# Conversion of the first feed-forward matrix in quarters, and other hand-over times for the start and the last two heads

## The chip, the cores and the metric

The kernel runs on one core of a Trainium2 chip. The metric is the device time of one execution in microseconds, the lower the better. The page and the trace are of one execution that the hardware profiler recorded. TensorE (PE) multiplies matrices, VectorE (DVE), ScalarE (ACT) and GpSimd (POOL) work on tiles in SBUF and PSUM, and SyncE (SP) issues the DMA transfers. PSUM has eight banks, and one matmul group fills one.

## What is computed

The input x is 16 sequences of 512 tokens with 256 features. A layer norm of x feeds an attention layer with 8 heads and a feed-forward net with three sign matrices, and both are added to x:

```python
def _L0_attn_ref(x, wq, wk, wv, wo):
    q, k, v = (einsum('bim,mhd->bhid', x, w) for w in (wq, wk, wv))
    q, k = rope(q), rope(k)
    s = einsum('bhid,bhjd->bhij', q, k) / 128
    s = s - 1e30 * (i < j)
    o = einsum('bhij,bhjd->bhid', softmax(s), v)
    return einsum('bhid,hdm->bim', o, wo)

def _L0_ffn_ref(x, k0, k1, k2, s0, s1, s2):      # k: booleans, True is 1 and False is -1
    h = concatenate([x, -x])                      # 256 -> 512 features
    h = relu(s0 * dense(k0, h)) * 2               # 512 -> 1024
    h = relu(s1 * dense(k1, h)) * 2               # 1024 -> 1024
    return s2 * dense(k2, h)                      # 1024 -> 256

xn = layernorm(x)
x = x + _L0_attn_ref(xn, ...) + _L0_ffn_ref(xn, ...)
```

## The kernel before

The kernel is one program of five instruction streams, written by Python code that runs once. Each stream is a `Queue` (L104), played in the order in which the code put things into it; an engine never takes a later instruction before an earlier one. Streams wait for each other by semaphores (`Queue.wait`).

**Units of work.** The batch entries b run from 0 to 15, and heads are counted through, g = 8 b + h, from 0 to 127. Every matmul group is a `Fill` (L467): it takes the PSUM bank that is planned to be free first, waits for the readers of what was in it, and issues its matmuls. For a head, `qk` (L585) makes q and k (two fills of 6 matmuls), `scores` (L636) the scores (three fills, 12 matmuls in all), `values` (L728) the product with v, called PV here (18 matmuls). Besides there are `v_proj`, `layer0`, `layer0_pair`, `layer1` (batch 0 only), the products of a Strassen scheme (`strassen`, L892) that take the place of layer 1 for the other batches, `layer2`, and the output projection (`proj`, `proj_last`). All numbers are kept as a high and a low f16 half, so most results are read twice: ACT makes the high half, DVE the low half by a subtraction.

**A head's chain behind its scores.** DVE adds the mask and takes the maxima (L659); ACT makes the bias (L667) and four exponentials, one for each 128 query rows (L673, tile p); DVE makes the inverse of the sums (L678, L680); POOL makes four high halves of the probabilities (L690, tile ph), DVE four low halves (L696, P_lo below); then SP issues two DMA transposes of ph into pt (`turned`, L699), and PV reads pt. For q and k, ACT swaps halves (L605, L606), DVE and POOL multiply by cos and sin, DVE adds (L618), ACT and DVE split (L624, L628).

**What sets the order.** PE's order is written by a loop over slots g (L1145): qk of head g + 2, then scores of head g + 1, then PV of head g - 1, with fillers between them. `PLACES` (L53) says for each filler its slot from the batch's first head and an order 0 to 5: 0 and 1 stand behind qk, 2 and 3 behind the scores, 4 and 5 behind PV. The order on the other engines follows from a clock that counts PE's work in units of a matmul of 512 columns: `at(delay, fn)` (L449) lets a step be written once the clock has moved by the delay. The delays are in `DELAY` (L96); the first three heads have their own in `EARLY` (L90), and steps that occur once at the start have absolute times in `SETUP` (L83). A step that someone needs earlier is pulled in front (`need`). `HELD` only guides the choice of banks.

**The start** (L1084). x of batch 0 is normalised on DVE, turned by PE into two banks (`first_T`, L548; eight matmuls of f32), and split by ACT and DVE into the tile xT. k0 arrives as bytes in the tile o. `subtract_k0` (L387, DVE) takes the difference of its halves for 512 of the 1024 columns into the fp8 tile w, and `sign_k0` (L394, ACT) multiplies by the sign of s0. `layer0(0, n)` (L763) multiplies the columns 128 n by xT; it waits for the half of w that it reads. `convert_k1` makes the 8 slices of the second matrix, five on POOL and three on ACT; `combine` (L419, POOL) and `block` (L411, ACT) make the seven fp8 operands WA of the Strassen scheme. `largest` and `powers` find powers of two by which the attention's weights are scaled, on DVE with two tiny matmuls each; `split_w` (ACT and DVE) then splits a part of a weight matrix. `last_load` (L258) is SP's wait for the differences of k0, since wo is loaded into the bytes' place.

## Time and profile before

| | us |
|---|---|
| median of 3 runs | 1779.78 |
| lowest and highest | 1779.66, 1780.92 |
| the profiled execution | 1781.45 |
| its span in the trace | 1779.6 |
| PE, DVE, ACT, POOL busy | 1723.5 (97%), 1535.5 (86%), 1269.1 (71%), 923.6 (52%) |
| chain that ended last: PE, DVE, DMA, ACT, POOL | 67%, 18%, 4%, 4%, 3% |

The profiled execution took 1.85 us more than its span, and it lies 1.67 us above the median. PE is busy nearly all the time, so the time is PE's work, at the clock it was granted, and the gaps in it. The timeline's rows give the start of a group of equal instructions, the time from its first start to its last end, and in brackets how long the engine had idled before and who ended that. Rows of a running group overlap by up to a tenth of a microsecond, since an engine takes the next instruction before the last has fully ended.

### The profile page before, as it was taken

To read this page: it belongs to the slowest core of one execution; us is meant where nothing else is said; L and a number is where in the kernel's file an instruction comes from. 1 tells how busy PE (TensorE), PEld (TensorE's weight loads), DVE (VectorE), ACT (ScalarE), POOL (GpSimd) and SP (SyncE) were. 2 spreads that over 40 slices of the span, in tenths; PEclk is the share of its full clock that TensorE was granted. 3 is DMA by queue.
4 is the path that set the end of the run, shared out by engine and by line. 5 is a ranking of instruction groups with operands and counts; after the bars stand their busy time and mean duration, and the time that the engine had idled before them with its cause. 6 is when DMAs were issued, how large, how long until landed. Compare 5 with 4: busy or idle time off the path is not lost.

```text
span 1779.6 us, 34027 instructions
## 1 busy us (share of the span) xinstructions
PE 1723.5 (97%) x12720; PEld 1196.4 (67%) x12720; DVE 1535.5 (86%) x3628; ACT 1269.1 (71%) x2715; POOL 923.6 (52%) x952
## 2 busy tenths in 40 slices
PE   6899989999999999999999999999999999999998
PEld 2456757767676676767767677676766767677667
DVE  8899888897988979898897988979889798888974
ACT  6777676777867678676776867778676776767773
POOL 6555544554545555455455545545455554555542
PEclk9999999999999999999999999999999999999999
DMA  5234543344343434334244433443533343343433
GB/s 171 48 55 72 94 68 78 66 82 80 55 96 63 80 66 72 78 66 96 56 87 73 66 78 66 84 78 55 96 66 78 66 72 82 63 95 59 80 65 66
DMA packets 454838, 134.08 MB, mean 75 GB/s; under 512 B 434704, under 2 KB 453648, under 8 KB 454672
## 3 DMA queue, kind: packets, MB, share of 16 engines
q1 hardware_dynamic: 454672, 131.90, 39.8%
q8 instruction: 100, 1.64, 0.4%
q14 instruction: 66, 0.54, 0.1%
HBM read 14.94 MB, written 8.39 MB: 13 GB/s over the span
## 4 chain that ended last, share of the span: by engine, by line
PE 67%; DVE 18%; DMA 4%; ACT 4%; POOL 3%; issue 3%; SPq 0%; DVEq 0%; POOLq 0%
PE bank L484 67%; DMA pt<-ph 3%; DVE ph L696 3%; DVE p L659 2%; DVE bank L618 2%; DVE bank L610 2%; DVE qk L628 2%; ACT p L673 2%; DVE rt L834 1%; DMA xT<-rt 1%; POOL tb L614 1%; POOL xT L316 1%; DVE v L538 1%; DVE hb L815 1%; DVE o L538 1%
## 5 line engine op out<-in xcount | busy, mean ns | idle before, releaser
L690 POOL TENSOR_SCALAR ph<-p,ri 128x384 f16<-128x384 f32 (+3 forms) x512 | 311.7, 609 | 453.5 <-DVE rk L680 416.2
L614 POOL TENSOR_TENSOR tb<-tb,sin 128x512 f32<-128x512 f32 x256 | 331.6, 1296 | 250.8 <-ACT tb L606 245.2
L484 PE MATMUL bank<-hb,wa 128*128 128x256 f16 x3360 | 379.7, 273 | 0.0
L484 PEld LDWEIGHTS bank<-hb,wa 128*128 128x128 fp8e5 x3360 | 328.0, 98 | 41.3
L673 ACT ACTIVATE p<-p,nm,sc 128x512 f32<-128x512 f32 (+3 forms) x512 | 328.6, 645 | 1.6
L696 DVE SCALAR_TENSOR_TENSOR ph<-p,rk,ph 128x512 f16<-128x512 f32 (+3 forms) x512 | 311.8, 616 | 0.0
L659 DVE CUSTOM_DVE_ANT_0 p<-bank,mask 128x512 f32<-128x512 f32 (+3 forms) x512 | 229.2, 485 | 51.1 <-PE bank L484 48.0
L484 PE MATMUL bank<-pt,v 128*128 128x256 f16 (+1 forms) x2304 | 234.0, 256 | 16.1 <-DMA pt<-ph 15.8
L484 PE MATMUL bank<-qk 128*128 128x512 f16 (+3 forms) x1536 | 231.4, 300 | 16.3 <-DVE qk L628 14.0
L484 PEld LDWEIGHTS bank<-pt,v 128*128 128x128 f16 x2304 | 203.3, 98 | 44.3 <-DMA pt<-ph 22.9
L484 PEld LDWEIGHTS bank<-qk 128*128 128x128 f16 x1536 | 133.3, 98 | 123.0 <-DVE qk L628 22.4
L624 ACT ACTIVATE qk<-bank 128x512 f16<-128x512 f32 x256 | 151.1, 591 | 78.2 <-DVE bank L618 77.8
L628 DVE TENSOR_TENSOR qk<-bank,qk 128x512 f16<-128x512 f32 x256 | 175.1, 684 | 29.5 <-ACT qk L624 28.2
L618 DVE TENSOR_TENSOR bank<-bank,tb 128x512 f32<-128x512 f32 x256 | 177.9, 695 | 17.3 <-POOL tb L614 12.4
L484 PE MATMUL bank<-wv,xT 128*128 128x512 f16 x768 | 183.7, 379 | 3.9 <-DMA xT<-rt 3.8
L605 ACT ACTIVATE tb<-bank 64x512 f32<-64x512 f32 x256 | 152.2, 594 | 49.3 <-PE bank L484 42.0
L484 PE MATMUL bank<-xT,wk 128*128 128x512 f16 x768 | 186.7, 379 | 0.3 <-DVE v L538 0.3
L484 PE MATMUL bank<-xT,wq 128*128 128x512 f16 x768 | 186.7, 379 | 0.0
L610 DVE TENSOR_TENSOR bank<-bank,cos 128x512 f32<-128x512 f32 x256 | 177.2, 692 | 5.0 <-ACT tb L606 4.9
L484 PE MATMUL bank<-wo,o 128*128 128x256 f16 x1536 | 173.1, 273 | 0.0
L844 POOL TENSOR_TENSOR hb<-rt,hb 128x1024 f16<-128x1024 f32 x60 | 132.3, 2205 | 61.7 <-ACT hb L840 60.5
L484 PEld LDWEIGHTS bank<-wo,o 128*128 128x128 f16 x1536 | 150.4, 98 | 20.6
(107 smaller groups left out, 2265.5 us busy)
## 6 DMA issues: line engine op xcount, KB each, us to landing
out<-xnat SPq DMA_DIRECT2D x32, 256.0 KB, 2.3
xnat<-in_x SPq DMA_DIRECT2D x15, 512.0 KB, 3.9
pt<-ph SPq DMA_TRANSPOSE x256, 4.3
o<-in_k SPq DMA_DIRECT2D x1, 1024.0 KB, 7.8
v<-in_wq SPq DMA_DIRECT2D x1, 1024.0 KB, 9.8
v<-in_wk SPq DMA_DIRECT2D x1, 1024.0 KB, 11.6
ph<-in_wv SPq DMA_DIRECT2D x1, 1024.0 KB, 14.0
o<-in_wo SPq DMA_DIRECT2D x1, 1024.0 KB, 10.8
```

Of the source, the lines that this page charges most:

```text
L484: self.todo.append(lambda e, stop=False: e.matmul(self.ps[:, cols[0]:cols[1]], lhsT, rhs, start=first, stop=stop, skip_group_check=skip))
L605: act.put(lambda e: e.activation(TB[0:64, r, :], f.ps[64:128, :], ACT.Copy))
L610: done["straight", n] = dve.put(lambda e: e.tensor_tensor(f.ps[:, :], f.ps[:, :], COS[:], ALU.mult))
L614: done["crossed", n] = pool.put(lambda e: e.tensor_tensor(tb, tb, SIN[:], ALU.mult))
L618: done["rot", n] = dve.put(lambda e: e.tensor_tensor(f.ps[:, :], f.ps[:, :], tb, ALU.add))
L624: done["qk_hi", n] = act.put(lambda e: e.activation(hi, f.ps[:, :], ACT.Copy))
L628: done["qk_lo", n] = dve.put(lambda e: e.tensor_tensor(lo, f.ps[:, :], hi, ALU.subtract))
L659: done["max", g, i] = dve.put(lambda e, i=i, a=a, w=w: e.tensor_tensor_reduce(out=P[:, r, S_OFF[i]:S_OFF[i] + w], in0=f.ps[:, a:a + w], in ...
L673: done["exp", g, i] = act.put(lambda e: e.activation(v, v, ACT.Exp, bias=NM[:, g % 4, i:i + 1], scale=SC[:, 0:1], accum_out=SM[:, g % 4, i ...
L690: done["P_hi", g, i] = pool.put(lambda e: e.tensor_scalar(part(r, i, HI), v, RI[:, g % 4, i:i + 1], 4096.0, ALU.mult, ALU.mult))
L696: done["P_lo", g, i] = dve.put(lambda e: e.scalar_tensor_tensor(part(r, i, LO), v, RK[:, g % 4, i:i + 1], part(r, i, HI), ALU.mult, ALU.su ...
L844: done["h0t", b, i] = pool.put(lambda e: e.tensor_tensor(HB[:, 3:7, LO, i, :], RT[:, 4:8], HB[:, 3:7, HI, i, :], ALU.subtract))
```

## The change

The edits are these.

1. k0 is converted in four quarters of 256 columns, each with its own event, in place of two halves. The signs of the three scales are made before the normalised x is written. The first quarter is subtracted right after that, and its sign is put on ACT between the first and the second high half of xT; the three others follow both halves of xT on DVE and on ACT. `layer0(0, n)` waits for quarter n // 2. SP's load of wo waits for all four differences.
2. `SETUP`, `EARLY` and the places of the fillers of batch 0, of a pair of layer 0 and two Strassen parts of batch 1, and of two fillers of the last batch have other numbers.
3. A table `LATE` gives the last two heads, 126 and 127, delays of their own for nine steps.

```diff
 PLACES = {
-    "l0_1": ((2, 2), (3, 0), (4, 4), (5, 2)),
+    "l0_1": ((2, 2), (3, 0), (3, 5), (5, 2)),
...
-    "seg_15": ((2, 0), (3, 4), (4, 1), (4, 2), (5, 2), (5, 2), (5, 5), (6, 5)),
+    "seg_15": ((2, 0), (3, 4), (4, 1), (4, 2), (5, 2), (5, 4), (5, 5), (6, 5)),
...
+LATE = dict(rotated=14.1, qhi=19.3, qlo=22.0, bias=4.9, exp=11.3, inv=19.6, high=36.1, low=33.0, turned=46.4)
...
-            sp.wait(done["k0_diff", 0], done["k0_diff", 1])
+            sp.wait(*[done["k0_diff", n] for n in range(4)])
...
+        def quarter(v, n):
+            return v.rearrange("p (c n) -> p c n", c=2)[:, :, n * 256:n * 256 + 256]
+
+        def subtract_k0(n):
 
             dve.wait(done["k_in", 0])
-            done["k0_diff", half] = dve.put(lambda e: e.tensor_tensor(
-                W0[:, :, half * 512:half * 512 + 512], halves(K0S[:, 0:2048], half), halves(K0S[:, 2048:4096], half),
+            done["k0_diff", n] = dve.put(lambda e: e.tensor_tensor(
+                W0[:, :, n * 256:n * 256 + 256], quarter(K0S[:, 0:2048], n), quarter(K0S[:, 2048:4096], n),
                 ALU.subtract, saturate=False))
 
+        def sign_k0(n):
+
+            act.wait(done["k0_diff", n], done["signs"])
+            w0 = W0[:, :, n * 256:n * 256 + 256]
+            done["W0", n] = act.put(lambda e: e.activation(w0, w0, ACT.Copy, scale=SG[:, 0:1], saturate=False))
...
-            return EARLY[name][g] if g < 3 and name in EARLY else DELAY[name]
+            if g < 3 and name in EARLY:
+                return EARLY[name][g]
+            return LATE[name] if g >= G - 2 and name in LATE else DELAY[name]
...
                 split(f, XT[:, 0, HI, :, c, :], XT[:, 0, LO, :, c, :], ("xT_hi", c), ("xT", 0, c))
+                if c == 0:
+                    at(DELAY["hi"], lambda: sign_k0(0))
...
-            pe.wait(done["W0", n // 4])
+            pe.wait(done["W0", n // 2])
...
         norm(0)
+        signs()
         norm_apply(0)
-        signs()
         subtract_k0(0)
-        sign_k0(0)
         ffn_scales()
-        subtract_k0(1)
-        last_load()
         first_T()
         while later:
             later.pop(0)[1]()
-        sign_k0(1)
+        for n in range(1, 4):
+            subtract_k0(n)
+            sign_k0(n)
+        last_load()
```

What the tables do to the order is seen on three engines.

The first place is ACT at the start, from the first conversion of k0 (w<-w,sg) to the first products of layer 1 (h<-bank). wa are the Strassen operands, wq and wk the first split parts of the weights. Before:

```order
L398 ACTIVATE w<-w,sg 128x2x512
L530 ACTIVATE xT<-bank 128x4x128 x2
L398 ACTIVATE w<-w,sg 128x2x512
L408 ACTIVATE hb<-o,sg 128x1024
L408 ACTIVATE rt<-o,sg 128x1024 x2
L530 ACTIVATE hb<-bank 128x512 x8
L416 ACTIVATE wa<-hb 128x1024
L416 ACTIVATE wa<-rt 128x1024
L530 ACTIVATE h<-bank 128x512
L360 ACTIVATE wq<-v,kn 128x2x256
L360 ACTIVATE wk<-v,kn 128x2x256
L416 ACTIVATE wa<-hb 128x1024 x2
```

and now:

```order
L535 ACTIVATE xT<-bank 128x4x128
L401 ACTIVATE w<-w,sg 128x2x256
L535 ACTIVATE xT<-bank 128x4x128
L401 ACTIVATE w<-w,sg 128x2x256 x3
L411 ACTIVATE hb<-o,sg 128x1024
L411 ACTIVATE rt<-o,sg 128x1024 x2
L535 ACTIVATE hb<-bank 128x512 x8
L419 ACTIVATE wa<-hb 128x1024
L419 ACTIVATE wa<-rt 128x1024
L419 ACTIVATE wa<-hb 128x1024 x2
L535 ACTIVATE h<-bank 128x512
L363 ACTIVATE wq<-v,kn 128x2x256
```

The first high half of xT stands ahead of any conversion, and three quarters stand ahead of the conversion of k1 (hb<-o,sg and rt<-o,sg) where one half stood. Two of the operands wa have moved ahead of h, wq and wk.

The second place is PE behind the PV of head 2 (bank<-pt,v; the last of its four rows is shown). xT,w is a pair of layer 0 of batch 1, w,h is layer 2 of batch 0, and xT,wq and xT,wk are q and k of head 6. Before:

```order
L484 MATMUL bank<-pt,v 128x128 x3
L484 MATMUL bank<-xT,wq 128x512 x6
L484 MATMUL bank<-xT,wk 128x512 x6
L484 MATMUL bank<-wv,xT 128x512 x6
...
L484 MATMUL bank<-w,h 128x256 x32
L484 MATMUL bank<-xT,w 128x512 x8
L484 MATMUL bank<-wv,xT 128x512 x6
```

and now:

```order
L489 MATMUL bank<-pt,v 128x128 x3
L489 MATMUL bank<-xT,w 128x512 x8
L489 MATMUL bank<-xT,wq 128x512 x6
L489 MATMUL bank<-xT,wk 128x512 x6
L489 MATMUL bank<-wv,xT 128x512 x6
...
L489 MATMUL bank<-w,h 128x256 x32
L489 MATMUL bank<-wv,xT 128x512 x6
```

The third pair of layer 0 has moved ahead of head 6's q and k. The rows left out end with the PV of head 3 in both.

The third place is DVE at the end, between the last inverse but one (head 126; ri and rk) and the maxima of head 127 (ISA p,mx). The ph rows are the P_lo, the two first here of head 125 and the four next of head 126; bank<-bank,rt and h<-bank,h belong to the Strassen scheme of batch 15, o<-bank,o to the PV of head 124. Before:

```order
L696 SCALAR_TENSOR_TENSOR ph<-p,rk,ph 128x256
L696 SCALAR_TENSOR_TENSOR ph<-p,rk,ph 128x128
L535 SCALAR_TENSOR_TENSOR h<-bank,h 128x2x256
L696 SCALAR_TENSOR_TENSOR ph<-p,rk,ph 128x512
L538 SCALAR_TENSOR_TENSOR o<-bank,o 128x512
L696 SCALAR_TENSOR_TENSOR ph<-p,rk,ph 128x384
L889 TENSOR_TENSOR bank<-bank,rt 128x512
L659 ISA p,mx<-bank,mask 128x512
...
L659 ISA p,mx<-bank,mask 128x256
L659 ISA mx 128x1
L535 SCALAR_TENSOR_TENSOR h<-bank,h 128x2x256
L696 SCALAR_TENSOR_TENSOR ph<-p,rk,ph 128x128
```

and now:

```order
L703 SCALAR_TENSOR_TENSOR ph<-p,rk,ph 128x256
L703 SCALAR_TENSOR_TENSOR ph<-p,rk,ph 128x128
L543 SCALAR_TENSOR_TENSOR o<-bank,o 128x512
L703 SCALAR_TENSOR_TENSOR ph<-p,rk,ph 128x512
L703 SCALAR_TENSOR_TENSOR ph<-p,rk,ph 128x384
L703 SCALAR_TENSOR_TENSOR ph<-p,rk,ph 128x256
L540 SCALAR_TENSOR_TENSOR h<-bank,h 128x2x256
L896 TENSOR_TENSOR bank<-bank,rt 128x512
L703 SCALAR_TENSOR_TENSOR ph<-p,rk,ph 128x128
L666 ISA p,mx<-bank,mask 128x512
```

The last P_lo of head 126, on which its DMA transposes wait, stood behind all four maxima of head 127 and two rows more, and stands ahead of the first of them now. On PE the PV of head 124 moves ahead of 32 matmuls of the Strassen scheme, and on ACT a copy of that scheme (bank<-bank, L875) moves from ahead of head 126's bias to between the high halves of q and the first exponential. Between the two ends, from head 9 to head 123, the rows of all five engines are the same in both kernels but for the numbers of the banks.

## Rows read from the trace of the kernel before

**Rows 1.** Three stretches: length, busy us per engine (count), granted clock, DMA share, GB/s.
```profile
0.00:170.00 170.00, 145.08 (x839) 80.67 (x840) 150.91 (x326) 122.74 (x240) 96.02 (x102) 0.97 0.38 87
170.00:1740.00 1570.00, 1544.67 (x11586) 1087.01 (x11585) 1367.16 (x3264) 1136.81 (x2454) 822.02 (x842) 1.00 0.41 74
1758.00:1760.00 2.00, 2.00 (x13) 1.51 (x12) 0.00 (x0) 0.00 (x0) 0.00 (x0) 0.50 0.00 0
```

**Rows 2.** Timeline of PE, last heads: start us, duration us, instructions, idle before them.
```profile
1747.56 1.82 PE L484 MATMUL bank<-pt,v 128*128 128x256 f16 x18
...
1750.96 3.66 PE L484 MATMUL bank<-w,h 128*128 128x256 fp8e5 x32
...
1757.15 3.32 PE L484 MATMUL bank<-pt,v 128*128 128x256 f16 x18 [2.53 <-DMA pt<-ph]
...
1760.26 6.92 PE L484 MATMUL bank<-wo,o 128*128 128x256 f16 x60
```

**Rows 3.** Timeline, the issue of the last three pairs of DMA transposes by SyncE.
```profile
1742.00 3.72 SPq L707 DMA_TRANSPOSE pt<-ph  x2
...
1750.24 3.74 SPq L707 DMA_TRANSPOSE pt<-ph  x2
...
1763.04 3.70 SPq L707 DMA_TRANSPOSE pt<-ph  x2
```

**Rows 4.** Timeline of ScalarE, VectorE and GpSimd between 1735 and 1750 us.
```profile
1735.60 0.58 ACT L875 ACTIVATE bank<-bank 128x512 f32<-128x512 f32 x1
...
1740.94 0.17 DVE L678 RECIPROCAL ri<-sm 128x4 f32<-128x4 f32 x1
...
1741.41 3.05 POOL L690 TENSOR_SCALAR ph<-p,ri 128x512 f16<-128x512 f32 x4 [1.28 <-DVE rk L680]
...
1742.82 0.83 DVE L696 SCALAR_TENSOR_TENSOR ph<-p,rk,ph 128x512 f16<-128x512 f32 x1
...
1749.87 0.34 DVE L696 SCALAR_TENSOR_TENSOR ph<-p,rk,ph 128x128 f16<-128x128 f32 x1
```

**Rows 5.** Timeline of the start: x transposed, k0's signs, the first matmuls, GpSimd's combinations.
```profile
7.45 1.94 PE L489 MATMUL bank<-ident,rt 128*128 128x128 f32 x8 [7.45 <-DVE rt L316]
...
9.72 1.15 ACT L398 ACTIVATE w<-w,sg 128x1024 fp8e5<-128x1024 fp8e5 x1 [7.50 <-DVE w L390]
...
10.77 1.06 ACT L530 ACTIVATE xT<-bank 128x512 f16<-128x512 f32 x2
...
12.25 9.13 PE L484 MATMUL bank<-xT,w 128*128 128x512 f16 x32 [2.86 <-DVE xT L538]
...
17.68 4.20 POOL L428 TENSOR_TENSOR wa<-hb 128x1024 fp8e5<-128x1024 f16 x2 [0.41 <-POOL hb L405]
```

**Rows 6.** Timeline, from the first powers of two to the maxima of wo and wv.
```profile
24.00 1.95 DVE L342 TENSOR_SCALAR dg<-ident,ar 128x2 f32<-128x2 f32 x1
...
28.09 2.35 POOL L428 TENSOR_TENSOR wa<-wa,hb 128x1024 fp8e5<-128x1024 fp8e5 x1
...
28.48 2.50 DVE L362 SCALAR_TENSOR_TENSOR wk<-v,kn,wk 128x512 f16<-128x512 f32 x1
...
35.20 2.28 DVE L322 TENSOR_REDUCE p<-ph 128x1 f32<-128x2048 f32 x1
...
37.53 0.80 PE L484 MATMUL bank<-ident,p 128*128 128x128 f32 x2 [3.72 <-DVE p L322]
...
38.12 5.33 PE L484 MATMUL bank<-hb 128*128 128x512 f16 x12
```

**Rows 7.** Timeline, heads 2 to 7, where a pair of layer 0 moves.
```profile
115.71 0.18 DVE L678 RECIPROCAL ri<-sm 128x4 f32<-128x4 f32 x1 [0.96 <-ACT p L673]
...
116.66 1.81 PE L484 MATMUL bank<-pt,v 128*128 128x256 f16 x18
...
132.15 1.82 PE L484 MATMUL bank<-pt,v 128*128 128x256 f16 x18 [0.78 <-DMA pt<-ph]
...
139.40 1.79 PE L484 MATMUL bank<-qk 128*128 128x512 f16 x12 [1.54 <-DVE ri L678]
```

19 lines of the change are left out of this document (6 added, 13 removed), and 28 rows, old and new, of the table PLACES.

## Prediction

> **What bounds the kernel now.** I read first the table of stretches [rows 1]. From 170 to 1740 us PE is busy for 1544.67 of 1570 us at a clock of 1.00, and there the change moves nothing: only PE's work could make that part shorter. In the first 170 us PE is idle for 170 - 145.08 = 24.9 us, while DVE is busy for 150.91. So the start is set by DVE, ACT and POOL as much as by PE, and a gap that is closed there can come back at the next one. The end is the other place. The timeline of PE's last heads [rows 2] shows one wait that nothing makes good later: PV of head 126 stands for 2.53 us until its DMA transposes have landed, starts at 1757.15 us, and PE works without a gap from there to its last matmul. After the wait PE runs at a granted clock of 0.50 [rows 1], its lower level of 1.2 GHz: the 18 matmuls of this PV take 3.32 us where those of head 125 took 1.82 [rows 2].
>
> **The end, part by part.** The transposes of head 126 are issued from 1750.24 us [rows 3], directly behind P_lo of its last tile, which starts on DVE at 1749.87 [rows 4]. All its high halves were ready by 1741.41 + 3.05 = 1744.46 [rows 4]. So some 5 us of DVE's order, not its inputs, lie between. In the new order that P_lo stands ahead of head 127's maxima.
>
> When it runs now: a copy of the Strassen scheme, 0.58 us at 1735.60 on ACT [rows 4], ran where ACT had nothing else to do. It now stands between the first high half and the exponentials of head 126, so these end 0.5 us later, the inverse moves from 1740.94 to 1741.4, and POOL's four high halves end at 1744.9. On DVE there follow the last two P_lo of head 125, the low half of o, three P_lo of head 126 (the first was 0.83 us), a low half of h1, and an addition that waits for ACT's third copy. I add these to 1741.4 and come to about 1746.0 us for the last P_lo, 3.9 us earlier. From the issue to the PV that waited, head 125 took 1747.56 - 1742.00 = 5.6 us and head 126 6.9 us [rows 2, 3]. The transposes then land at 1751.9 to 1753.3.
>
> When PE comes: layer 2 starts at 1750.96 and takes 3.66 us [rows 2], so PE was ready for this PV at 1754.6. The late exponentials cost something here. The two late P_lo of head 125 move its transposes by 0.45 us, and since its PV followed them directly, PE comes 0.45 us later to all that follows; the copy that opens the next Strassen part costs about the same 0.5 us at the same place, and the two waits overlap. So PE comes at 1755.05, with 1.7 us in hand at worst. The wait of 2.53 us goes.
>
> With it goes the slow clock: 3.32 - 1.82 = 1.50 us on this PV, and, until the clock is back, an estimated 0.17 us on the first of the 60 matmuls behind it (6.92 us) [rows 2]. Sum: -2.53 - 1.50 - 0.17 + 0.45 = -3.75 us. What is late next is PV of head 127. Its transposes were issued at 1763.04 in a kernel that was 2.1 us behind, and only its last P_lo waits now for the low half of o of head 126, which follows PV by 2.4 us. That gives an issue near 1758.3 and a landing at 1763.9 to 1765.2, for a PV that PE reaches at about 1766.5 behind its projection and layer 2. The cover is 1.3 us at worst. Bounds of this part: 0 if the hand-over fails, -4.2 if the 0.45 us is not paid.
>
> **k0 in quarters.** The turned x leaves PE at 7.45 + 1.94 = 9.39 us, but ACT took a half of w (1.15 us) first and began on xT at 10.77; the first matmul waited for xT's low half until 12.25 [rows 5]. Now ACT begins near 9.5. A high half is 1.06 / 2 = 0.53 us; a quarter of w I take as half of 1.15, 0.6 us, with 1.15 as its upper bound if all of it were fixed cost. DVE's low half of about 0.6 us then ends near 10.8, and PE starts at 10.9: 1.35 us earlier. Behind that the lead shrinks. ACT now has three quarters in front of k1's conversion where it had one half, so its part of k1 ends near 17.6 us and not 16.3, and the high halves of the first layer start there. The seventh fill of layer 0 reuses the bank of the first and waits for that. PE ends layer 0 some 0.8 us earlier, not 1.35. POOL's combinations need all eight slices of k1, and began at 17.68 [rows 5], so they stay where they are or move by 0.1.
>
> And POOL pins what follows. A scaling of two columns on DVE (dg, L342) took 1.95 us, and the low half of the first part of wk 2.50 us [rows 6], while a POOL combination ran from 28.09 for 2.35 us; neither ended before POOL's instruction did. These two stand in the chain to the largest value of wv, which DVE finds at 35.20 to 37.48, and for which PE waits 3.72 us [rows 6]. If DVE reaches dg or wk 0.5 us earlier, it waits 0.5 us longer for the same POOL instruction. I take 0 for the whole lead at 37.5 us, between +0.3 (POOL moves) and -2.1, one POOL instruction less in the chain.
>
> The Trainium skill states this as a rule, in "SBUF — State Buffer", in its section "SBUF: two separate sides": DVE and GpSimd share one pair of ports as an exclusive lock, held for the whole instruction, and the loser fully blocks. By it the lead of 1.35 us is worth nothing as long as POOL's row of combinations stands still, and the trace agrees (2.50 us for wk). If the two shared bandwidth instead, the sum at 37.5 us would be about -0.8.
>
> **The other numbers at the start.** Two of ACT's fp8 operands move into a gap of ACT; q's part 2 and 3 of wq, the third low half of qk, wo's low halves and the low half of h1 change places on DVE. DVE is busy from 48.9 to 74 us but for its waits on POOL and ACT, and the same instructions stand in front of every wait of PE but the next two; I take 0, between +0.5 and -0.7, one low half (about 0.7 us) earlier in front of the scores of head 1.
>
> **The pair of layer 0** comes earlier on PE by the scores of head 5, PV of head 3 and layer 2. DVE's 0.96 us of idleness at 115.71 [rows 7] stays, since it waits there for ACT. The pair's two banks are freed only by DVE's last low half of it. With ACT's two rows and DVE's four differences and two low halves behind the inverse of 115.71 that is at 119.9 us. PV of head 3 takes one of these banks. It ran at 116.66 [rows 7] and, behind the pair's 8 matmuls (12 of the scores took 1.79 us), would now come at 118.4, so it gets a wait of 1.5 us that is not there today. P_lo of head 4 come 1.2 us later, so PV of head 4, at 132.15 after 0.78 us of waiting, waits until 133.4. But the scores at 139.40, which waited 1.54 us [rows 7], do so for DVE: in front of them stands the same work but one P_lo of 128 columns (0.34 us for such a one in [rows 4]), so they come at 139.0. PE's delay is absorbed there. I take -0.45 for the start as a whole, between +2 and -3.
>
> **The sum.** The profiled execution took 1781.45 us. It becomes 1781.45 - 3.75 - 0.45 = 1777.25. The median of the runs is 1.67 us lower, so the forecast is 1775.6 us, 0.24% less. A measurement of this kernel tells apart about 0.2%, 3.56 us.
>
> **Rivals.**
> *The start takes part of it back.* The new wait of PV 3 and the longer one of PV 4 are not absorbed, because ACT, too, is fuller behind the pair. 1.5 + 1.2 us of waits less the 0.45 above give +1 to +2 there, and 1777.5 us (1776.3 to 1778.8). For it: DVE is the fuller engine in this stretch, and nothing in the row at 139.40 shows how ACT stands. Against: the same work stands in front of 139.40.
> *A new wait at the end.* The hand-over is moved, and the 18 matmuls wait for another thing: the transposes of head 127, whose cover is only 1.3 us, or a larger loss at head 125. With the slow clock once more that gives back 2 to 3 us: 1778.3 us.
> *More than forecast.* DVE's dg slips in front of a POOL instruction, the maximum of wv comes up to 2 us earlier, and PE's wait of 3.72 us shrinks so far that the clock stays up behind it. Then the 12 matmuls at 38.12, which took 5.33 us behind the wait [rows 6], take about half of that. I take 2.5 us off in all: 1773.1 us.
> *Slower than before.* PV 3's wait is longer than I think, 4 us or more, because the pair's last low half is queued behind the maxima of head 5; PE falls to 1.2 GHz behind it as at 1757, and the chains of heads 5 and 6 start later by as much. It decides from a loss of 3.75 us at the start: 4 us of wait and 1.5 us of slow clock leave +1.75, 1781.5 us.
>
> The Trainium skill, "TensorE: Matmul & The Clock Gate", section "HAM oscillation — how this bites in real kernels", describes a kernel in which each wait for a DMA sends the matmuls behind it to half clock. Here the waits of 3.72 and 2.53 us agree with it, and that of 1.54 us does not show it. [...]
>
> **How the numbers follow.** Forecast 0.42, with its own range 1774.3 to 1777.0; start takes part back 0.28; new wait at the end 0.12; more than forecast 0.13; slower 0.05. Faster by over 3.56 us, below 1776.2: most of the first (0.39), all of the fourth (0.13), a little of the second (0.03), 0.55. Slower by over 3.56 us: 0.03. Within: 0.42. The range runs from 1772.8 to 1778.7: it leaves out the slower case, half of the new wait, and the lower part of the fourth, 0.17 together.
>
> **What would show it.** Right: no idle time before the PV of head 126, its 18 matmuls in 1.8 us, the issue of its transposes near 1746 us on today's scale; the first matmul of layer 0 at 10.9 us, the wait for the maximum of wv ending at 37.5 +- 0.3 us; a wait of some 1.5 us before PV 3. The prediction is wrong if PE waits at head 125 or 127 for over 1 us, if the maximum of wv comes before 36.5, or if the scores of head 7 start after 140 us.

## The result, and the profile after

The changed kernel takes 1774.49 us (median of 7 runs, 1773.84 to 1776.89), the kernel before 1779.78 us (7 runs, 1777.15 to 1780.92). The ratio is 0.9973, with a 95% interval of 0.9962 to 0.9985: 5.3 us less, where 4.2 were forecast. The profiled execution took 1775.91 us and has a span of 1774.1 us.

The stretches of [rows 1] in the kernel after (the third is now the one in which the PV of head 126 runs):

```profile
0.00:170.00 170.00, 142.64 (x842) 79.72 (x843) 149.72 (x329) 122.73 (x243) 98.09 (x102) 0.99 0.39 88
170.00:1740.00 1570.00, 1545.06 (x11599) 1088.13 (x11598) 1368.40 (x3265) 1136.41 (x2456) 821.83 (x842) 1.00 0.41 74
1753.00:1755.00 2.00, 2.00 (x24) 1.83 (x22) 1.49 (x3) 0.00 (x0) 1.24 (x3) 1.00 0.00 0
```

PE is idle for 170 - 142.64 = 27.4 us of the first 170 (24.9 before) and yet has got further by then, since less of its work fell into stretches at 1.2 GHz. The end, on PE, as in [rows 2]:

```profile
1746.41 1.81 PE L489 MATMUL bank<-pt,v 128*128 128x256 f16 x18
...
1753.31 1.81 PE L489 MATMUL bank<-pt,v 128*128 128x256 f16 x18
1754.95 6.71 PE L489 MATMUL bank<-wo,o 128*128 128x256 f16 x60
...
1764.99 1.81 PE L489 MATMUL bank<-pt,v 128*128 128x256 f16 x18
```

The wait before the PV of head 126 is gone, and its 18 matmuls take 1.81 us. The chain ahead of it, as in [rows 3, 4] (GpSimd's high halves, DVE's last low half P_lo, and SyncE's transposes of heads 126 and 127):

```profile
1740.29 3.85 POOL L697 TENSOR_SCALAR ph<-p,ri 128x512 f16<-128x512 f32 x4 [1.59 <-DVE rk L687]
...
1745.10 0.34 DVE L703 SCALAR_TENSOR_TENSOR ph<-p,rk,ph 128x128 f16<-128x128 f32 x1
...
1745.47 3.70 SPq L714 DMA_TRANSPOSE pt<-ph  x2
...
1756.77 3.72 SPq L714 DMA_TRANSPOSE pt<-ph  x2
```

The start, as in [rows 5, 6]. ScalarE's signs of the quarters, DVE's subtractions, GpSimd's five slices of k1 and its row of combinations, and the chain to the maximum of wv:

```profile
10.64 7.37 PE L489 MATMUL bank<-xT,w 128*128 128x512 f16 x24 [1.29 <-DVE xT L543]
...
11.50 2.76 DVE L393 TENSOR_TENSOR w<-o 128x512 fp8e5<-128x512 uint8 x3
...
13.09 1.95 ACT L401 ACTIVATE w<-w,sg 128x512 fp8e5<-128x512 fp8e5 x3 [2.23 <-DVE w L393]
...
10.16 7.36 POOL L408 TENSOR_SCALAR hb<-o,sg 128x1024 f16<-128x1024 uint8 x5 [3.35 <-DMA o<-in_k]
18.61 4.21 POOL L431 TENSOR_TENSOR wa<-hb 128x1024 fp8e5<-128x1024 f16 x2 [1.09 <-ACT rt L411]
...
26.83 2.12 POOL L431 TENSOR_TENSOR wa<-hb,rt 128x1024 fp8e5<-128x1024 f16 x1
29.03 2.35 POOL L431 TENSOR_TENSOR wa<-wa,hb 128x1024 fp8e5<-128x1024 fp8e5 x1
...
24.31 0.51 DVE L345 TENSOR_SCALAR dg<-ident,ar 128x2 f32<-128x2 f32 x1
...
27.22 2.29 DVE L365 SCALAR_TENSOR_TENSOR wq<-v,kn,wq 128x512 f16<-128x512 f32 x1 [0.79 <-ACT wq L363]
29.43 2.50 DVE L365 SCALAR_TENSOR_TENSOR wk<-v,kn,wk 128x512 f16<-128x512 f32 x1
...
38.48 0.80 PE L489 MATMUL bank<-ident,p 128*128 128x128 f32 x2 [3.72 <-DVE p L325]
39.06 4.16 PE L489 MATMUL bank<-hb 128*128 128x512 f16 x12
```

And PE at heads 3, 4 and 7, as in [rows 7]:

```profile
120.43 1.80 PE L489 MATMUL bank<-pt,v 128*128 128x256 f16 x18 [1.40 <-DVE hb L822]
...
133.87 1.82 PE L489 MATMUL bank<-pt,v 128*128 128x256 f16 x18 [0.89 <-DMA pt<-ph]
...
139.41 1.79 PE L489 MATMUL bank<-qk 128*128 128x512 f16 x12
```

**Where the time went.** The start of each head's PV in PE's timeline serves as a time mark along the kernel. The table gives it for one profiled execution of each kernel, in us against the kernel before (minus is earlier), with the duration of the PV of head 126 in brackets where it was slow. The experiments below stand in the same table. Medians and ratios are against runs of the kernel before on the same chip: its medians there were 1780.05 us (end_only, start_only, plo_back, k1_first), 1780.46 us (quarters_only, pair_back, warm, fetch) and 1779.90 us (the last four rows).

| kernel | head 0 | 7 | 12 | 17 | 123 | 125 | 126 | 127 | median us | ratio, interval |
|---|---|---|---|---|---|---|---|---|---|---|
| before, absolute | 83.37 | 164.35 | 229.53 | 302.49 | 1727.79 | 1747.56 | 1757.15 (3.32) | 1770.51 | 1779.78 | |
| after | +0.42 | -0.60 | -0.57 | -0.87 | -1.43 | -1.15 | -3.84 | -5.52 | 1774.49 | 0.9973, 0.9962 to 0.9985 |
| end_only | -0.07 | -0.08 | +0.03 | -0.09 | -0.75 | -0.46 | -3.16 | -4.83 | 1776.97 | 0.9988, 0.9979 to 0.9997 |
| start_only | +0.15 | -0.85 | -0.74 | -0.81 | -1.11 | -1.14 | -1.14 (2.91) | -1.15 | 1778.50 | 0.9996, 0.9988 to 1.0005 |
| plo_back | -1.35 | -2.37 | -2.25 | -2.52 | -3.61 | -3.33 | -3.44 (3.38) | -3.44 | 1777.81 | 0.9991, 0.9982 to 1.0000 |
| quarters_only | -0.90 | -0.88 | -0.77 | -0.82 | -1.10 | -1.13 | -1.13 (3.31) | -1.29 | 1780.03 | 0.9998, 0.9988 to 1.0007 |
| pair_back | -0.05 | -0.05 | -0.03 | -0.33 | -1.18 | -0.90 | -3.60 | -5.27 | 1776.30 | 0.9978, 0.9969 to 0.9987 |
| k1_first | -1.71 | -2.73 | -2.66 | -2.86 | -2.38 | -2.08 | -4.77 | -6.44 | 1774.72 | 0.9973, 0.9964 to 0.9982 |
| warm | -1.17 | -2.23 | -2.19 | -5.15 | -4.03 | -3.74 | -6.44 | -8.11 | 1772.68 | 0.9961, 0.9948 to 0.9973 |
| fetch | +0.14 | +0.14 | +0.16 | -3.16 | -5.59 | -5.62 | -6.93 | -8.59 | 1772.71 | 0.9957, 0.9944 to 0.9971 |
| whole_block | -0.44 | -0.40 | -0.30 | -0.17 | -0.16 | -0.19 | -0.16 (3.19) | -0.45 | 1780.63 | 1.0007, 0.9998 to 1.0016 |
| after_44 | -1.44 | -2.44 | -2.41 | -4.00 | -5.68 | -5.39 | -8.08 | -9.75 | 1770.92 | 0.9950, 0.9934 to 0.9965 |
| k1_44 | +0.48 | -0.56 | -0.55 | -3.66 | -6.15 | -5.86 | -8.55 | -10.23 | 1769.65 | 0.9946, 0.9934 to 0.9959 |
| k1_88 | -0.17 | -0.13 | -0.03 | -1.62 | -2.00 | -0.83 | -3.53 | -5.20 | 1775.76 | 0.9973, 0.9963 to 0.9982 |

Of the 5.52 us that the kernel after is ahead at head 127, 0.60 were gained by head 7, 0.83 between heads 7 and 123, where the rows are the same from head 9 on, and 4.09 behind head 123.

### The profile page after: what moved, and what is told of

Same layout as the page of the kernel before. It is cut to its first block, busy times and chain, and to the rows that moved or that the text cites. A ratio compares the mean times of both kernels' runs of the same rounds, so it can differ in the third digit from the quotient of the medians.

```text
span 1774.1 us, 34030 instructions
## 1 busy us (share of the span) xinstructions
PE 1718.2 (97%) x12720; PEld 1194.3 (67%) x12720; DVE 1534.4 (86%) x3630; ACT 1267.5 (71%) x2717; POOL 925.6 (52%) x952
## 3 DMA queue, kind: packets, MB, share of 16 engines
q8 instruction: 100, 1.64, 0.4%
## 4 chain that ended last, share of the span: by engine, by line
PE 67%; DVE 19%; ACT 5%; DMA 3%; POOL 3%; issue 2%; SPq 0%; DVEq 0%; POOLq 0%; ACTq 0%
PE bank L489 67%; DVE ph L703 3%; DVE p L666 3%; DVE bank L625 3%; DVE bank L617 2%; DVE qk L635 2%; DMA pt<-ph 2%; ACT p L680 2%; DVE rt L841 1%; POOL xT L319 1%; DVE v L543 1%; DMA xT<-rt 1%; POOL tb L621 1%; DVE hb L822 1%; DVE o L543 1%
## 6 DMA issues: line engine op xcount, KB each, us to landing
v<-in_wk SPq DMA_DIRECT2D x1, 1024.0 KB, 10.9
o<-in_wo SPq DMA_DIRECT2D x1, 1024.0 KB, 10.2
```

## The experiments

**Two halves of the change.** end_only is the kernel before with the table LATE (its line of numbers is left out of the cut) and these places; start_only is the kernel after without all of them:

```diff
-    "seg_15": (..., (5, 2), (5, 2), (5, 5), (6, 5)),
+    "seg_15": (..., (5, 2), (5, 4), (5, 5), (6, 5)),
-    "l2_15": ((8, 0), (7, 0)),
+    "l2_15": ((8, 2), (7, 0)),
-            return EARLY[name][g] if g < 3 and name in EARLY else DELAY[name]
+            if g < 3 and name in EARLY:
+                return EARLY[name][g]
+            return LATE[name] if g >= G - 2 and name in LATE else DELAY[name]
```

> The kernel before with only the change at the end: the table of distances for the last two heads, and the new places of the second Strassen scheme and of layer 2 in the last batch. The start is that of the kernel before. Theory: the end is worth the same without the new start, since nothing ties the two: no wait before the PV of head 126, its 18 matmuls in 1.8 us and not 3.3, and PE's end 4.1 us earlier counted from the PV of head 123 (2.69 of wait, 1.68 of slow clock, less 0.28 that the exponentials cost). In time 3.8 to 4.2 us less than the kernel before, ratio 0.9977. Rival: part of it comes from the start, in that the heads arrive at the end in another rhythm; then the wait stays over 0.5 us and the ratio is above 0.9985.

Measured: from head 123 to 127 PE gains 4.08 us, as in the kernel after (4.09). The wait is gone, so the rival falls. The median is 3.1 us lower, but the interval of the ratio (0.9979 to 0.9997, or 0.5 to 3.7 us) reaches neither the 4.1 us of the profile nor the ratio of 0.9977 that was forecast. The kernel before spreads from 1776.8 to 1781.8 us here. It may be that its faster executions lose less at the end than the profiled ones do; none of those was profiled, so this is not shown.

> The changed kernel without the end: last two heads, Strassen scheme and layer 2 of the last batch as in the kernel before. Theory: only the start's share remains, 0.6 to 0.9 us by the PV of head 17 (PE at 301.6), and a ratio of 0.9995 (0.9990 to 1.0). The wait of 2.5 us and the 3.3 us of the 18 matmuls at head 126 are back. Between the PVs of heads 17 and 121 the rows are the same in every kernel, so what these 1399 us differ by is scatter of single executions. Rival: the 0.76 us that the changed kernel gained there comes from its start (another phase of the transfers against the engines); then this kernel shows 1398.6 to 1398.7 there once more and the kernel with the new end alone 1399.4.

Measured: 0.85 us by head 7 and 0.81 by head 17, median 1.6 us lower, and the wait of head 126 and its slow matmuls are back. The middle, from head 17 to 121, took 1399.42 us before, 1398.66 after, 1398.77 in end_only, 1398.87 here, 1398.50 in plo_back and 1399.61 in k1_first. That follows neither the start nor the end, so the 0.8 us that the kernel after gained there is scatter of single executions. The two halves add up within such scatter: 3.1 + 1.6 us against 5.3 us.

**One instruction.** plo_back is the kernel after with the last P_lo of head 126 back behind the maxima of head 127:

```diff
-                at(delay("low", g) + n * DELAY["low_i"], lambda i=i: low(i))
-            at(delay("turned", g), turned)
+                at(delay("low", g) + n * DELAY["low_i"] + (10 if g == G - 2 and i == 0 else 0), lambda i=i: low(i))
+            at(delay("turned", g) + (10 if g == G - 2 else 0), turned)
```

> The changed kernel with one DVE instruction moved back: the last low half of P of head 126 stands behind the maxima of head 127 and one low half of h1 again, 0.34 us of work. Theory: this one instruction carries the gain at the end. It starts near 1748.6 us instead of 1745.1, its transposes are issued at 1748.9 and land 5.5 us later at the earliest, so the PV that PE reaches at 1753.3 waits for at least 1.1 us; with the slower landings that the kernel before shows (5.1 and 6.0 us per transpose) for 2.7 us and at 1.2 GHz, 4.1 us in all. Rival: the wait at head 126 came from the whole row of DVE or from ACT's copy ahead of the exponentials; then this kernel is within 0.5 us of the changed one.

The timeline of DVE, SyncE and PE, and then, from the view of tile pt, the landings of these two transposes (least, median and most us from issue):

```profile
1746.34 0.34 DVE L703 SCALAR_TENSOR_TENSOR ph<-p,rk,ph 128x128 f16<-128x128 f32 x1
...
1746.71 3.77 SPq L714 DMA_TRANSPOSE pt<-ph  x2
...
1753.71 3.38 PE L489 MATMUL bank<-pt,v 128*128 128x256 f16 x18 [2.42 <-DMA pt<-ph]
```

```profile
DMA to landing us min/median/max: 5.2/5.7/6.1
```

The wait is 2.42 us and the PV slow; from head 123 to 127 nothing is gained. In this order of the instructions the place of one instruction of 0.34 us, with the transposes that must follow it, decides on the whole gain at the end. It also left a question: the two transposes landed 6.1 and 5.2 us from issue, and those of the kernel after 4.3 and 3.8.

**Why they land late.** The DMA engines in 40 slices of 0.2 us, before (1750 to 1758 us), with the queues in the half microsecond from 1754.0:

```profile
DMA  0000000799999999999999990000006990000000
GB/s 0 0 0 0 0 0 0 151 223 215 209 209 212 220 220 216 212 193 192 205 220 291 129 29 0 0 5 9 9 9 146 289 200 0 0 0 0 0 0 0
...
q8 instruction: 1, 0.02, 11.7%
```

At slice 21, counted from 0, one packet of 16 KB with instructions passes (q8, with its MB and its share). The transposes had moved some 210 GB/s; from slice 23 on they move 0 to 29 for seven slices, 1.4 us. The kernel fetch has 44 more matmuls on PE while it waits for x; whole_block has 128:

```diff
             fs = [Fill(("T", c)) for c in range(2)]
+            for _ in range(44):
+                pe.put(lambda e: e.matmul(fs[0].ps[:, 0:2], ID[:].bitcast(F16)[:, 0:128],
+                                          ID[:, 0:2].bitcast(F16)[:, 0:2], start=True, stop=True), signal=False)
```

> The kernel before with 44 matmuls of 2 columns more on PE, in the 7.4 us in which it waits for x; they are not read. They move nothing but PE's place in its own instruction stream, by 88 instructions. Theory: the transposes of head 126 landed late (5.1 and 6.0 us from issue, where others need 3.6 to 4.3), because a block of PE's instructions was loaded at 1754.4 us over the same DMA engines: from 1754.5 to 1756 they moved 4 to 37 GB/s and not 204. Here that block is loaded about 5 us earlier, between the transposes of heads 125 and 126. Then they land 3.6 to 4.3 us from issue, and the wait before the PV of head 126 is 1.0 to 1.3 us and not 2.53. Rival: the late landing comes from the place, for instance from what else runs there; then the landings stay at 5.1 and 6.0 us and the wait at 2.5.

The same views of fetch, 7 us earlier in the execution (1743 to 1751 us), and its PV of head 126:

```profile
DMA  0020000000000069999999999999999981000000
GB/s 0 0 82 0 0 0 0 0 0 0 0 0 0 0 146 223 211 211 210 223 210 220 223 212 188 200 200 229 210 207 223 201 168 18 0 0 0 0 0 0
```

```profile
DMA to landing us min/median/max: 3.8/4.1/4.3
```

```profile
1750.22 1.82 PE L484 MATMUL bank<-pt,v 128*128 128x256 f16 x18 [1.22 <-DMA pt<-ph]
```

and the PV of head 13, before and in fetch:

```profile
244.29 2.59 PE L484 MATMUL bank<-pt,v 128*128 128x256 f16 x18 [3.50 <-DMA pt<-ph]
```

```profile
243.16 1.82 PE L484 MATMUL bank<-pt,v 128*128 128x256 f16 x18 [2.21 <-DMA pt<-ph]
```

The packet passes ahead of the transposes of head 126 (slice 2). These run through and land 3.8 and 4.3 us from issue, PE waits 1.22 us, and the clock stays up. The kernel before has become 7.7 us faster, by instructions that compute nothing. In the profile 3.0 us of this lie at the end (head 123 to 127). Another 3.3 us lie between heads 12 and 17, where the wait for the transposes of head 13 fell from 3.50 to 2.21 us and 1.7 us of slow clock behind it went. These two transposes landed 5.5 and 6.0 us from issue before, with a packet of instructions at 241.5 to 242 us and 1 GB/s in the half microsecond behind it, and 4.2 and 4.3 us from issue here. The last 2.4 us lie in the middle, and no run takes them apart. The next packet now meets the transposes of head 127, which land 5.0 and 6.2 us from issue; PE comes to them late enough and does not wait.

> The kernel before with 128 matmuls of 2 columns more on PE at the start, where 44 gave 7 us. Theory: the loads of PE's instructions come in equal blocks: 100 of them with 1.64 MB for PE's some 25,500 instructions in the kernel before, so one per about 256. 128 matmuls with their weight loads are 256 instructions, so all later loads fall where they fell in the kernel before. The transposes of head 126 land 5.1 and 6.0 us from issue again, PE waits 2.5 us for them, at head 13 it waits 3.5 us, and the ratio is 1.000 (within 0.0008). Rival: the 44 matmuls helped in another way (PE is busy before its first work, the clock, the first rows); then 128 help as much or more, ratio 0.996.

PE at heads 13 and 126, and the landings at head 126:

```profile
243.98 3.08 PE L484 MATMUL bank<-pt,v 128*128 128x256 f16 x18 [3.49 <-DMA pt<-ph]
...
1756.99 3.19 PE L484 MATMUL bank<-pt,v 128*128 128x256 f16 x18 [2.57 <-DMA pt<-ph]
```

```profile
DMA to landing us min/median/max: 5.1/5.6/6.2
```

256 instructions more, and both waits are back. So the added matmuls do not help by themselves; it is the place of the loads that counts, and they repeat every 256 instructions of PE: 100 packets of 16 KB go with the 25,440 matmuls and weight loads of the kernel before, and 101 with those of whole_block. The Trainium skill says the same of the block ("Runtime: NRT & Kernel Launch", section "Instruction fetch mechanics": 16 KiB, 256 instructions), but calls the cost of crossing it mostly hidden. Here it is not hidden where transposes are in flight and PE waits for them: 1.4 us. The two heads are no exception. Of the 1792 pairs of transposes in the 14 profiles, the 986 with no packet of instructions of 8 KB or more in flight have landed 5.5 to 5.8 us from the issue of the first of the two; of the 478 with one of PE's packets over 1 us behind the issue, half need some 6.8 us or more, and the slowest 7.7.

after_44 is the changed kernel with the 44 matmuls of fetch:

> The changed kernel with the 44 matmuls of 2 columns at the start. Theory: the load that made the transposes of head 126 late in the kernel before no longer counts here, since the hand-over is 4 us earlier; what the shift still gives is the part ahead of the last heads: 3.3 us at heads 12 to 15, where PE waits 3.46 us for the transposes of head 13 and then runs at 1.2 GHz, and 2.4 us in the middle, 5.7 in all. So about 1769 us, ratio 0.994. At the end no wait before the PV of head 126. Rival: the loads now fall on other transposes that had no slack in this kernel, the end among them; then less than 3 us are left against the changed kernel.

Measured: 1770.92 us, 3.6 us under the changed kernel. Between heads 7 and 17 it gains 1.56 us (the PV of head 13 still takes 2.74 us behind a wait of 2.26 us), not 3.3; up to head 123 another 1.68 us. At the end nothing waits, and it gains the same 4.07 us over the kernel before as the changed kernel did. One step of the theory did not hold: a load falls on the transposes of head 126 again, 3.2 us behind their issue, and they land 4.7 and 5.6 us from issue. But the last has landed at 1747.67 us, 1.4 us before PE comes to their PV at 1749.07. So the early P_lo covers the load too. The gain ahead of the last heads is there, but its size was put too high.

**The start.** quarters_only is the kernel before with the part of the change that the diff shows in `subtract_k0`, `sign_k0`, `first_T`, `layer0` and behind `norm(0)`, and all tables old. Of it, in short:

```diff
-        sign_k0(1)
+        for n in range(1, 4):
+            subtract_k0(n)
+            sign_k0(n)
```

> The kernel before with k0 in four quarters and nothing else: all tables are the old ones. Theory: the first matmul of layer 0 is at 10.65 us, and ScalarE's conversions of k1 end after 18 us, so GpSimd's row of combinations starts at 18.4 to 18.9 and not at 17.68; with it DVE's low half of wk ends at 30.0 to 31.9 us, by whether DVE or GpSimd gets in first. In the old order an h1 half and a cosine product stand before the maxima of wv too. The wait for the maximum of wv ends within 1 us of 37.53, and by the PV of head 17 PE is within 0.5 us of the kernel before. Rival: the start's gain of 0.6 to 2.5 us comes from the quarters alone; then it is 0.6 us ahead or more.

Measured: GpSimd's row starts at 19.26 us and not by 18.9, the wait for the maximum of wv ends at 37.15, PE is 0.88 us ahead at head 7 and 0.82 at head 17, and the median is 0.4 us lower, which is no difference. The profile sides with the rival on the size; the times tell nothing apart. PE from the maximum of wv on:

```profile
37.15 0.49 PE L484 MATMUL bank<-ident,p 128*128 128x128 f32 x2 [3.72 <-DVE p L322]
37.47 2.75 PE L484 MATMUL bank<-hb 128*128 128x512 f16 x12
...
45.84 0.59 PE L484 MATMUL bank<-dg,p 128*128 128x2 f32 x2 [3.45 <-DVE dg L342]
```

Behind the same wait of 3.72 us that was followed by 1.2 GHz in [rows 6], the clock stayed up here (2.75 us for the 12 matmuls), with the microseconds coming back as a longer wait for dg (3.45 us; 1.12 in the kernel before).

pair_back is the kernel after with the old place of the third pair of layer 0:

```diff
-    "l0_1": ((2, 2), (3, 0), (3, 5), (5, 2)),
+    "l0_1": ((2, 2), (3, 0), (4, 4), (5, 2)),
```

> The changed kernel with the third pair of layer 0 of batch 1 in its old place, behind the layer 2 of batch 0. Theory: the pair's place is worth 1.0 us: from the PV of head 0 to that of head 7 the changed kernel gained 1.02 us (from +0.42 to -0.60 against the kernel before), in spite of a new wait of 1.40 us before the PV of head 3. With the pair back that wait is gone, the scores of head 7 wait for 1.5 us again, and the distance from the PV of head 0 to that of head 7 is 80.98 us as in the kernel before, and not 79.96. Rival: that gain comes from the other numbers (exponentials, low halves), and the pair's place gives 0; then it is 79.9 to 80.2.

Measured: 80.98 us from head 0 to head 7, as before; after, start_only, plo_back and after_44 have 79.96 to 79.98. The pair's place is worth 1.0 us, its new wait included.

k1_first is the kernel after with ScalarE's slices of k1 partly ahead of the signs:

```diff
+        convert_k1(act, 5, 7)
         for n in range(1, 4):
             subtract_k0(n)
             sign_k0(n)
...
-        convert_k1(act, 5, 8)
+        convert_k1(act, 7, 8)
```

> The changed kernel with two of ScalarE's three slices of k1 converted ahead of the signs of quarters 1 to 3 of k0, where ScalarE stood idle for 2.23 us because the subtraction of quarter 1 on DVE took 1.56 us beside a conversion on GpSimd. Theory: GpSimd's row of combinations needs all eight slices of k1; it began at 18.61 in the changed kernel, 0.93 later than before, and everything that DVE does beside it moved with it, so that the wait for the maximum of wv ended at 38.48 and not at 37.53. Here ScalarE is done with k1 at 16.5, GpSimd starts the row at 17.55 behind its own slices, 1.06 earlier, and the wait for the maximum of wv ends at 37.4. By the PV of head 17 PE is 0.5 to 1.1 us ahead of the changed kernel; ratio to the kernel before 0.9968. Rival: DVE and GpSimd share and don't block each other; then GpSimd's row moves by 1.06 us, but the maximum of wv by less than 0.3 us, since DVE's own work is the same.

GpSimd's slices and row, and the two low halves on DVE, here and in start_only:

```profile
10.64 7.38 POOL L408 TENSOR_SCALAR hb<-o,sg 128x1024 f16<-128x1024 uint8 x5 [3.82 <-DVE xT L543]
18.43 4.21 POOL L431 TENSOR_TENSOR wa<-hb 128x1024 fp8e5<-128x1024 f16 x2 [0.41 <-ACT hb L535]
...
26.65 2.57 POOL L431 TENSOR_TENSOR wa<-hb,rt 128x1024 fp8e5<-128x1024 f16 x1
...
26.25 0.98 DVE L365 SCALAR_TENSOR_TENSOR wq<-v,kn,wq 128x512 f16<-128x512 f32 x1 [0.79 <-ACT wq L363]
27.16 2.60 DVE L365 SCALAR_TENSOR_TENSOR wk<-v,kn,wk 128x512 f16<-128x512 f32 x1
```

```profile
11.10 7.37 POOL L405 TENSOR_SCALAR hb<-o,sg 128x1024 f16<-128x1024 uint8 x5 [4.27 <-DMA o<-in_k]
...
27.10 2.62 POOL L428 TENSOR_TENSOR wa<-hb,rt 128x1024 fp8e5<-128x1024 f16 x1
...
26.98 0.75 DVE L362 SCALAR_TENSOR_TENSOR wq<-v,kn,wq 128x512 f16<-128x512 f32 x1 [0.80 <-ACT wq L360]
27.65 2.62 DVE L362 SCALAR_TENSOR_TENSOR wk<-v,kn,wk 128x512 f16<-128x512 f32 x1
```

The forecast start of the row at 17.55 us failed: GpSimd's own five slices of k1 take 7.4 us and end at 18.02. In 13 of the 14 profiles the row starts 0.41 us behind them, as in [rows 5], so ScalarE is not what it waits for; the exception is the profiled execution of the kernel after, in which the slices began at 10.16 us, the earliest of all (the row at 18.61, behind 1.09 us of waiting for ScalarE). The ratio came out near the forecast (0.9973 for 0.9968), but not by the step that was to give it. So the edit is worth nothing that is shown: k1_44, with the same code, is at +0.48 at head 0 where k1_first is at -1.71. What the rows do show is how GpSimd pins DVE, that is, holds up an instruction of DVE until its own has ended. The low half of wk ends 0.55 us behind the end of GpSimd's instruction in all 14 profiles: 29.76 behind 26.65 + 2.57 = 29.22 here, 30.27 behind 29.72 in start_only, 31.93 behind 31.38 in the kernel after, 30.98 behind 30.44 in [rows 6]. In the new order DVE comes to these two while GpSimd's fifth combination is about to begin, and it is decided by some tenths of a microsecond whether wq's low half gets in ahead of it (0.75 to 0.98 us) or is pinned too (2.29 us in the kernel after), and with it whether PE gets the maximum of wv at 36.3 to 37.2 or at 38.48.

**The clock at the start.** warm is k1_first with 14 matmuls on PE ahead of the wait for the maximum of wv, in `turn_largest`; their results are not read:

```diff
+            for _ in range(14 if i == 2 else 0):
+                pe.put(lambda e: e.matmul(f.ps[:, 0:512], W0[:, 0, 0:128], XT[:, 0, HI, :, 0, :], start=True,
+                                          stop=True), signal=False)
```

> The kernel of the run before with two slices of k1 ahead, and 14 matmuls of 512 columns more on PE (3.2 us at full clock) in its wait of 3.7 us for the maximum of wv; their results go to a bank that is written anew and are not read. Theory: what the start is worth is decided by the slow clock behind this wait, which differs between executions: the 12 matmuls behind it took 5.33, 4.16, 4.29 and 4.44 us in four profiles, and 2.75 where PE had not waited. With PE busy during the wait the clock stays up: 2.75 us, 1.4 to 2.6 us gained there, and the scores of head 1 in 1.8 us. By the PV of head 17 PE is 1 to 1.7 us ahead of the run without them; ratio to the kernel before 0.9962. Rival: DVE sets the pace behind it, and the 1.7 us come back as longer waits for dg and qk before the scores of heads 0 to 2; then nothing is left at the PV of head 17 (within 0.3 us).

```profile
32.73 3.19 PE L333 MATMUL bank<-xT,w 128*128 128x512 f16 x14
36.62 0.49 PE L493 MATMUL bank<-ident,p 128*128 128x128 f32 x2 [0.70 <-DVE p L325]
36.94 2.75 PE L493 MATMUL bank<-hb 128*128 128x512 f16 x12
...
45.09 0.59 PE L493 MATMUL bank<-dg,p 128*128 128x2 f32 x2 [3.23 <-DVE dg L349]
45.54 5.28 PE L493 MATMUL bank<-hb 128*128 128x512 f16 x12
```

The clock stays up (2.75 us) and the gain is given back at the next hand-over: PE waits 3.23 us for dg where k1_first waits 1.72, and runs at 1.2 GHz behind that (5.28 us for 12 matmuls). x arrived 0.47 us later in this execution; taking that off, the PV of head 0 is at -1.64 against -1.71. So the rival was right on the start, and quarters_only shows the same without added matmuls. At head 17 warm is 2.3 us ahead of k1_first all the same, where the rival had 0 and the theory 1 to 1.7, and its ratio (0.9961) met the forecast (0.9962) by luck. All of these 2.3 us come behind head 12, and the wait of head 13 is 2.30 us with a PV that is not slow, as in fetch. It fits that the 28 further instructions move the loads; this was not separated by a run of its own.

**A version faster than both.**

> The kernel with two slices of k1 ahead of k0's signs, with the 44 matmuls of 2 columns at the start. Theory: both gains add up, since the one lies before head 7 and the other behind it: its PV of head 7 is 1 to 2.7 us ahead of the kernel before, and from there the distances are those of the changed kernel with the 44 matmuls; about 1768.5 us, the fastest so far, ratio 0.9935. Rival: the start's gain of this kernel is only the scatter of single executions; then it takes the same time as the changed kernel with the 44 matmuls, within 0.5 us.

The edit is that of k1_first with that of fetch; k1_88 has `range(88)` in its place. Measured: 1769.65 us (5 runs, 1768.71 to 1771.19), 10.2 us (0.54%) under the kernel before; its distance to after_44 is 1.3 us with ranges that overlap, so it is not shown that the edit at the slices adds anything. At head 7 the profile is 0.56 us ahead of the kernel before, as the kernel after is, and not 1 to 2.7 as forecast.

> The same with 88 matmuls instead of 44, which puts the loads of PE's instructions another 88 instructions ahead, some 5.5 us. Theory: only the place of the loads differs, and there are some 100 of them against 256 transposes, so the time moves by one to four us in either direction, and the waits before the PVs of heads 13 and 126 are those of a landing in 3.6 to 4.3 us unless a load falls on them. Rival: the number of added matmuls doesn't matter once it isn't zero; then it is within 0.5 us of the run with 44.

Measured: 6.1 us slower than with 44, more than the forecast one to four. Loads now fall on other transposes: those of head 5 land 4.9 and 6.0 us from issue (3.5 and 4.3 in the kernel after) and its PV waits 1.74 us (0.39); those of head 125 meet a packet at 1742.2 us, and the wait for them is new, as the row shows:

```profile
1746.73 1.82 PE L489 MATMUL bank<-pt,v 128*128 128x256 f16 x18 [0.72 <-DMA pt<-ph]
```

The number of added instructions matters, and the rival falls.

## Why the prediction was right, step by step

**The end: right, by its own working, and beside a cause it had not seen.** P_lo was forecast 3.9 us earlier and comes 3.3 us earlier against PE (1745.10 + 1.43 for the lead at head 123, against 1749.87). The wait of 2.53 us went; from the PV of head 126 to that of 127 it is 11.68 and not 13.36 us, 1.68 for the clock where 1.50 + 0.17 stood. The late exponentials cost 0.28 and not 0.45 us (-1.43 at head 123, -1.15 at 125). The sum is 4.09 instead of 3.75 us. The transposes of head 127 are issued 8.2 us ahead of its PV, as forecast. What the prediction took as a property of the hand-over, a landing 6.9 us from issue, was a block of instructions on the same DMA engines. With that out of the way (fetch) the old order loses 1.2 us and no clock, and the new order then gives 1.07 us more (fetch against after_44, head 123 to 127). The two remedies overlap. Moving the load away gives 3.0 of the 4.09 us; moving P_lo alone gives all of them, with the load out of the way (the kernel after) or on the transposes (after_44).

**The quarters: first step right, second wrong.** PE starts at 10.64 us (forecast 10.9). But "POOL's combinations ... stay where they are or move by 0.1" failed: the row starts at 18.4 to 19.3 us in the ten kernels with quarters, and at 17.6 to 17.9 in the four with halves. The sum had counted what the three quarters do to ScalarE and not what their subtractions do to GpSimd: behind 11.5 us they lie beside its slices of k1, which take 7.3 to 7.4 us instead of 5.9 to 6.5. Slice by slice, four of the five take 1.2 us each, and one, which runs while DVE subtracts, takes 2.6 to 2.7 us (in quarters_only two are longer, 2.21 and 1.61; in the kernel before the first, 1.81 beside the second half's subtraction). In fetch and whole_block, where the subtractions are over by the start of the slices to within 0.1 us, none is longer than 1.20. ScalarE idles for 1.9 to 2.2 us until the first of these subtractions is done (2.23 in the profile after), so that it ends k1 at 18.1 to 18.4 and not at 17.6.

**The maximum of wv: mechanism right, number wrong.** "37.5 +- 0.3" was 38.48 in the profiled execution and 36.7 to 36.8 in start_only, plo_back, pair_back and after_44, which run the same code there. The pin by GpSimd is what sets it, as said. The lower bound's "one POOL instruction less in the chain" is what happens in most executions, at wk: its low half ends behind GpSimd's fifth combination there, and behind the sixth in the kernel before and the kernel after. The rival that saw dg slip in front of a POOL instruction named the wrong place. dg did slip (0.51 us in the kernel after, 1.95 before), and the maximum came 0.95 us later even so. The Trainium skill's rule ("SBUF — State Buffer", section "SBUF: two separate sides"), by which DVE is blocked for the whole of GpSimd's instruction, agrees with the end of wk's low half in all 14 profiles.

**The pair: right.** The new wait before the PV of head 3 is 1.40 us (1.5), the PV of head 4 comes at 133.87 (133.4), the scores of head 7 wait for nothing and come at 139.41 (139.0) behind a start that is 0.4 us late. Its worth is 1.0 us, where the sum had 0.4.

**The start as a whole** was put at -0.45 us. It is -0.60 in the profiled execution, and that this is so near is luck: +0.42 at head 0, where about 0 stood, and -1.02 from there to head 7, where -0.4 stood, happen to add up so. It is -0.85 in start_only and -2.4 in plo_back and after_44, which have the same start, and the median of start_only is 1.6 us lower. Much of this scatter is the clock: start_only and plo_back reach the maximum of wv within 0.12 us of each other and are 1.5 us apart at the next wait, since the 12 matmuls behind the first took 5.33 us in one and 4.29 in the other. Below 4.4 us hardly anything more is gained: from the maximum of wv to dg warm, with 2.75 us, takes 8.47 us and k1_first, with 4.44, takes 8.64. **The middle**, put at 0, is 0 within its scatter. In the profiled executions the change gave 5.5 us where 4.2 were forecast, and 0.8 of the 1.3 us between them are that scatter.

Of the rivals, the slower one did not occur: PE's wait at head 3 stayed at 1.4 us and the clock stayed up. "A new wait at the end" did not either; the cover of head 127 is 2.7 us and not 1.3.

## What to carry to other kernels

Before a late DMA transpose is put down to its issue, look at the DMA rows at that place for a packet of instructions: here two such places cost 6.3 us (before against fetch), more than the whole change gained, and 88 instructions of no meaning at an idle place moved them away. A hand-over with slack is the other remedy: the transposes of head 126 in after_44 and of head 127 in fetch met a load and nothing waited. Where a kernel is tuned by its order, the place of PE's instruction blocks is part of what is tuned, and any edit that adds or removes PE instructions changes it. And a step that is cut into parts is to be costed on every engine that its parts now lie beside, not only on the one that waits for it.

## What the runs showed of the hardware

- One block of PE's instructions (16 KB, one per 256 instructions) stops transposes in flight for some 1.4 us: 0 to 29 GB/s where 210 were moved. The landing goes from 3.5 to 4.4 us to 4.9 to 6.2 us. Seen at head 126 in before, start_only, plo_back, quarters_only and whole_block, at head 13 in before and at head 5 in k1_88, and absent at heads 13 and 126 in fetch.
- Waits of 1.22 us (head 126 in fetch) and 1.74 us (head 5 in k1_88) left the clock at 2.4 GHz: the PV behind them took 1.82 us. Waits of 2.42 to 2.57 us before the PV of head 126 and of 3.38 to 3.55 us before that of head 13 were each followed by 1.2 GHz, and those of 2.2 to 2.3 us at head 13 by either (1.82 us in fetch, k1_44 and warm, 2.74 and 2.71 us in after_44 and k1_88; the granted clock is 1.00 from 243 to 245 us in fetch and 0.50 from 242 to 244 us in after_44).
- Behind the wait of 3.7 us for the maximum of wv, 12 matmuls took 4.1 to 5.3 us in twelve profiles and 2.75 us in one (quarters_only). With 14 matmuls that fill that wait they took 2.75 us too (warm). Both times the microseconds came back as waiting for DVE at the next hand-over (3.45 and 3.23 us).
- DVE and GpSimd hold each other up. A conversion of a slice of k1 on GpSimd took 2.6 to 2.7 us beside DVE's subtractions and 1.2 without them, and a low half of wq on DVE that began 0.4 us behind GpSimd's combination took 2.29 us (the kernel after) where one that began 0.12 us ahead of it took 0.75 (start_only).
